# Perceiver block on one core: each batch's context loaded in two halves and its keys in two groups, each behind an event of the running batch

## What is computed

```python
def xattn(x, context, W_out, b_out, heads=16):      # keys and values are both the context itself
    q = heads_of(x); k = v = heads_of(context)
    attn = softmax(einsum('bhid,bhjd->bhij', q, k) * 32 ** -0.5)
    return merge(einsum('bhij,bhjd->bhid', attn, v)) @ W_out.T + b_out

x = x + xattn(layernorm(x), ctx_1024, W_out, b_out)
x = x + attn(layernorm(x), ...)    # latent self-attention: low-rank q and kv, rotary part, 16 heads
x = x + ffn(layernorm(x), ...)     # 8 experts, each token takes the one with the largest gate
```

## Time and profile before

| | us |
|---|---|
| median of 3 runs | 781.83 |
| lowest and highest of them | 777.88, 782.9 |
| the profiled execution, its time | 780.07 |
| its span, first to last instruction | 778.2 |
| granted clock of TensorE, mean of the span | 0.98 |

### The profile page before, as it was taken

How to read it: one execution, slowest core, us unless ns; L and a number is a source line. 1 busy time by engine, 2 the same in 40 slices (tenths; PEclk the granted TensorE clock), 3 DMA queues, 4 the chain that set the end, 5 groups by cost and what they waited for, 6 DMA issues and landing times. The chain is left out here.

```text
span 778.2 us, 26293 instructions
## 1 busy us (share of the span) xinstructions
PE 704.4 (91%) x10502; PEld 550.8 (71%) x10502; DVE 582.8 (75%) x1184; ACT 429.5 (55%) x1085; POOL 336.0 (43%) x687
## 2 busy tenths in 40 slices
PE   5899889998999999979999899999886879999997
PEld 4546668787787787868878778788775656666664
DVE  4467587887988878868888797886556647788883
ACT  3344466674766666647666576674323545555552
POOL 1122353543354435334353435443315257866542
PEclk9999899999999999989999999999998899999999
DMA  8994445545556456454664555631613996544420
GB/s 277 296 234 101 132 142 159 178 143 152 162 155 194 143 159 184 140 141 147 170 183 143 164 164 152 181 122 28 232 41 103 366 393 242 170 154 140 146 97 5
DMA packets 114378, 129.07 MB, mean 166 GB/s; under 512 B 14479, under 2 KB 81295, under 8 KB 114257
## 3 DMA queue, kind: packets, MB, share of 16 engines
q1 hardware_dynamic: 108192, 111.12, 48.2%
q0 software_dynamic: 5520, 16.26, 6.0%
q10 hardware_dynamic: 544, 0.00, 0.0%
HBM read 114.77 MB, written 14.42 MB: 166 GB/s over the span
## 5 line engine op out<-in xcount | busy, mean ns | idle before, releaser
L918 ACT ACTIVATE prob<-scores,negmax 128x257 f32<-128x257 f32 x256 | 118.3, 475 | 106.1 <-DVE negmax L1118 106.1
L1373 POOL COPY plast<-prob 128x2 f32<-128x2 f32 x128 | 24.1, 189 | 210.4 <-ACT prob L918 209.0
L560 PE MATMUL stage_banks<-qkv_hi,operand_hi 128*128 128x398 f32 x256 | 100.3, 392 | 0.2 <-DVE operand_lo L1122 0.2
L561 PE MATMUL stage_banks<-qkv_lo,operand_hi 128*128 128x398 f32 x256 | 89.0, 348 | 2.1 <-issue 2.1
L562 PE MATMUL stage_banks<-qkv_hi,operand_lo 128*128 128x398 f32 x256 | 89.1, 348 | 0.0
L1118 DVE TENSOR_REDUCE negmax<-scores 128x2 f32<-128x514 f32 x128 | 82.5, 686 | 8.7 <-PE scores L626 8.7
L1108 DVE STREAM_TRANSPOSE k_t<-keys 128x512 f32<-128x512 f32 x128 | 82.6, 685 | 2.6 <-DMA keys<-in_ctx 2.6
L1670 PE MATMUL stage_banks<-w_all,hidden 128*128 x184 | 82.8, 592 | 0.6 <-ACT hidden L1723 0.6
L636 PE MATMUL scores<-consts,prob 128*128 128x128 f32 x512 | 78.6, 278 | 1.4 <-ACT prob L918 1.0
L1766 DVE TENSOR_TENSOR w_lo<-w_all,w_hi 128x512 fp32r<-128x512 f32 x89 | 75.4, 906 | 0.2
L1113 DVE COPY prob_t<-scores 128x512 f32<-128x512 f32 x64 | 43.1, 674 | 39.5 <-PE scores L636 39.5
(11 more groups left out here) (262 smaller groups left out, 1649.5 us busy)
## 6 DMA issues: line engine op xcount, KB each, us to landing
keys<-in_ctx SPq DMA_DIRECT2D x256, 128.0 KB
context<-in_ctx SPq DMA_DIRECT2D x64, 512.0 KB, 4.0
w_all<-in_L_ffn_W SPq DMA_DIRECT2D x16, 1024.0 KB, 10.9
b<-in_L_ffn_b SPq DMA_DIRECT2D x23, 256.0 KB
norm_scratch<-norm SPq DMA_DIRECT2D x16, 256.0 KB, 3.2
x_tile<-in_x SPq DMA_DIRECT2D x8, 256.0 KB, 2.9
x_pair<-in_x SPq DMA_DIRECT2D x8, 256.0 KB, 3.0
x_scratch<-x_tile SPq DMA_DIRECT2D x8, 256.0 KB, 2.2
```

The lines of the kernel that those rows point to most:

```text
L560: pe.matmul(to, op_hi[op][:, c, :], w_hi[name][:, c, columns], start=(c == 0), stop=False)
L561: pe.matmul(to, op_hi[op][:, c, :], w_lo[name][:, c, columns], start=False, stop=False)
L918: act.activation(prob[pair][:, gg, :], scores[:, g, 0:J], ACT.Exp, bias=negmax[b % 2][:, g:g + 1], accum_out=sums[t % 2][:, g, bl:bl + 1]) ...
```

## The change

`load_context` is cut in two by partitions (64 rows of partitions each, 256 KB), and each half adds 16 to the semaphore, so `attend` waits for 32 a use. `load_keys` takes a list of the groups it is to load. In SP's loop a batch b has now: at k = 2 the first half of the context of b + 3 (behind batch b - 1 attended, as before), at k = 4 its second half (behind the exponentials of the first pair of batch b), at k = 6 two of the four DMAs of keys of b + 2 (behind all exponentials of batch b), and at k = 8 the other two (behind both turned probabilities of batch b). The wait for the keys of b to be turned stays. The loads before the loop keep their order, with eight halves of context in place of four whole ones.

```diff
-KEYS_LOAD_AT = 1
+CONTEXT_LOAD_AT, KEYS_LOAD_AT = (2, 4), (6, 8)
...
         def load_context(b):
             until.wait_ge(attended, 2 * (b - 4) + 2)
+            for half in range(2):
+                load_context_half(b, half)
+
+        def load_context_half(b, half):
+            rows = slice(half * P // 2, (half + 1) * P // 2)
             src = ins["ctx_1024"][b, 0:C2 * P, :].rearrange("(p c) d -> p c d", c=C2)
-            sp.dma_start(context[b % 4][:, :, :], src).then_inc(context_loaded[b % 4], 16)
-
-        def load_keys(b):
+            sp.dma_start(context[b % 4][rows, :, :], src[rows, :, :]).then_inc(context_loaded[b % 4], 16)
+
+        def load_keys(b, places=range(HL)):
             until.wait_ge(keys_turned, 2 * (b - 2) + 2)
-            for hl in range(HL):
+            for hl in places:
...
-            if k == 2 and 1 <= b and b + 3 < B:
-                load_context(b + 3)
-            if k == KEYS_LOAD_AT and 1 <= b and b + 2 < B:
-                load_keys(b + 2)
+            if k == CONTEXT_LOAD_AT[0] and 1 <= b and b + 3 < B:
+                until.wait_ge(attended, 2 * b)
+                load_context_half(b + 3, 0)
+            if k == CONTEXT_LOAD_AT[1] and 1 <= b and b + 3 < B:
+                until.wait_ge(exped, 4 * b + 2)
+                load_context_half(b + 3, 1)
+            if k == KEYS_LOAD_AT[0] and 1 <= b and b + 2 < B:
+                until.wait_ge(exped, 4 * b + 4)
+                load_keys(b + 2, (0, 1))
+            if k == KEYS_LOAD_AT[1] and 1 <= b and b + 2 < B:
+                until.wait_ge(prob_turned, 2 * b + 2)
+                load_keys(b + 2, (2, 3))
...
-            until.wait_ge(context_loaded[b % 4], 16 * (b // 4 + 1))
+            until.wait_ge(context_loaded[b % 4], 32 * (b // 4 + 1))
```

## The result

The changed kernel takes **807.4 us** (median of 4 runs, 805.1 to 811.0), the kernel before 782.4 us beside it (4 runs, 777.9 to 784.3): 1.034 times as long, with an interval of 1.030 to 1.039. It is slower by 25 to 27 us, and the time lies far above the range of 775 to 790.5 us. The profiled execution took 806.8 us, with a span of 805.0.

What follows compares the result with a forecast made beforehand. The prediction took PE to bound the kernel, with slack in the loads. Halves and loop keys cost 0 and batch 3's keys 1.0 us: 780.07 + 1.0 = 781.1 us, put at 782.0 towards the runs' median, range 775 to 790.5.

Steps and rivals of the forecast that it cites:

- What bounds the kernel: Attention loop: PE sets the time, busy 405.5 of 440 us, DVE and ACT close behind; the loads have slack.
- Halves, cost 0: Context loads: over 20 us of lead in the loop; four more issues before it hidden, otherwise 1.3 us.
- The keys of batch 3, 1.0 us: Preparation: two key loads behind ten small loads; DVE waits 2.6 us, PE loses 0.8, bounds 0 to 2.8, taken 1.0.
- Second, first and third batches' keys: Loop: keys land before DVE turns them, margins 1.0 us (second), 3.1 (first), no less for the third; cost 0.
- Fourth batch's keys, late by 0.4 us and covered: Loop: four key loads land 0.4 us late, hidden by 1.26 us of DVE idle; cost 0, uncovered 6 us.
- y - 4.1: Loop: cost per tile of the fourth batch's keys for a landing of y us, after DVE's idle time is used.
- keys late in the loop: Rival, slower: landing of 4.5 us instead of 3.2 costs 9.8 us, 790.9; at 5.3, 32 us; chance 0.17.
- The stalls: Rival, faster: PE's "issue" stalls in the loop go, up to 7.4 us back, 773.7; chance 0.20.
- Nothing moves: Rival, preparation: other slack takes up PE's 0.8 us or small loads land sooner, 780.1 us; chance 0.13.
- knot: Loop, once a tile: fourth batch's four key loads in a row behind the normed x2's store; forecast cost 0.
- What would show it: Profile signs: DVE waits 2 to 4 us near 46 us, in the loop at most 0.5 a tile; over 1 refutes.

Runs made afterwards that it cites:

- e2: Kernel before with only the contexts loaded in 64-partition halves, keys as before: 793.5 us, ratio 1.012.
- e8: Kernel that only loads contexts, no computing: whole ones at 380 GB/s, pairs of 64-partition halves at 226, pairs of column halves at 358.
- e3: Changed kernel, but each context half is 2 KB of all 128 partitions instead of 64 whole partitions: 797.5 us, ratio 1.017 to the kernel before.
- e4: Changed kernel, but the four contexts ahead of the loop are loaded whole: 798.7 us, ratio 1.017 to the kernel before.
- e7: Kernel before, with only batch 3's keys in two groups, the second behind the ten small loads: 784.2 us, ratio 1.003.
- e5: Changed kernel, but each tile's second batch from tile 1 issues the fourth batch's keys early, at step 1: 791.4 us, ratio 1.017 to the kernel before.
- e1: Kernel before with only the keys moved to their new places, contexts loaded whole: 797.2 us, ratio 1.015.
- e10: Kernel before, with batch 3's four key loads at step 17 instead of 12, still ahead of the small loads: 780.8 us, ratio 0.998.
- e9: Kernel before, with only the fourth batch's keys moved late, in two groups behind the normed x2's store: 790.2 us, ratio 1.012.
- e6: Kernel before with contexts in column halves (2 KB of all 128 partitions), keys as before: 781.9 us, ratio 1.001.

## Why the prediction was wrong, point by point

**What bounds the kernel** was read rightly: PE's loop with slack in the loads, and that the change could use up that slack. The size of the slack was what mattered, and it was taken too large in three places.

**Halves, cost 0: the step that failed outright.** It counted an extra issue (at most 1.3 us, at 0.33 us each where a half's took 0.50 in the median) and the lead of 20 us in the loop. The lead is real: in e2 the loop loses nothing. But the step never priced the bytes of a half. Ahead of the loop there is no lead, since the queue is full and the weights stand behind the contexts, and there a load that takes nearly the time of a whole one for half the bytes delays everything behind it. Four contexts stand ahead of Wu_v; at 2.25 us each for 1.28 (e8) they take 3.9 us more, which is nearly half of the 8.5 us by which that weight landed later. The other half is not taken apart. e2 puts the whole at 9.5 us (1.012), e3 and e4 at 9 to 14 from the other side, e8 shows the rate itself. The trace of before had only whole contexts, so a bound was wanted here and none was given.

**The keys of batch 3, 1.0 us.** Place and mechanism were right: DVE waits from 45.3 us on (e7), and PE behind it. bias_out landed at 49.1 us, as forecast. The wait was mis-sized, 5.2 us for 2.6: the last key load landed 1.4 us behind bias_out and not with it (the upper bound allowed 2), and DVE came to it 1.1 us sooner than in the kernel before. PE lost 3.3 to 3.7 us for 0.8. In time it is worth 2.5 us alone (e7), and in the changed kernel nearly nothing is left of it beside the slower halves, where DVE waited 0.9 us. This is the term that the sum was built on, and the smallest of the three.

**Second, first and third batches' keys, margins of 1.0 us and more** held. Their landing was 3.43 us in the middle and the forecast 3.2, and DVE waited for none of them but once, for 0.5 us.

**Fourth batch's keys, late by 0.4 us and covered: the step that failed in the loop.** The order was as forecast, timeline of SP of the changed kernel:

```profile
288.40 0.34 SPq L472 DMA_DIRECT2D x_tile<-in_x  x1
288.78 0.43 SPq L552 DMA_DIRECT2D norm_scratch<-norm  x1
289.31 2.64 SPq L464 DMA_DIRECT2D keys<-in_ctx  x4
292.37 1.81 SPq L457 DMA_DIRECT2D context<-in_ctx  x2
```

and DVE behind it:

```profile
297.02 1.31 DVE L1121 STREAM_TRANSPOSE k_t<-keys 128x512 f32<-128x512 f32 x2 [3.01 <-DMA keys<-in_ctx]
298.25 0.65 DVE L1126 COPY prob_t<-scores 128x512 f32<-128x512 f32 x1
```

The idle time of 1.26 us ahead of the move of the probabilities is gone: that instruction follows at once. The last issue began at 291.34 and landed at 297.0, 5.7 us. The number that was wrong is the landing, 3.2 us from the start of the kernel where 5.38 was the median in the loop. It wasn't the only landing on record either: in the loop of the kernel before, the same trace's semaphore events have 3.74 us in the middle, and 4.02 for the fourth batch's keys, already ahead of the change. With 5.38 the prediction's own formula, y - 4.1, gives 1.28 us a tile; the loop lost 1.35 against e5, of which about 1.0 is left without the "issue" stalls. That it comes so close is partly luck: in e1 the formula gives 0.88 where 1.1 was lost against the kernel before, in e3 0.81 where 0.2 was. So the rival "keys late in the loop" had the mechanism, was right about the fourth batch's keys to within some 0.6 us a tile, and was given 17 in 100 on the strength of one landing. Its upper end of 5.3 us was a median in truth. The prediction leaned on four key loads being small; behind 512 KB of other traffic they landed later than a context's median of 4.0.

**The rivals.** The stalls did not go: 5.0 + 2.3 + 2.2 + 1.3 us for 5.3 + 2.1, which is 3.4 us more and over the 3 us that the prediction had named as a sign against it. They aren't shown to come from the change: over the 12 tiles they sum to 7.4 us in the kernel before, 9.2 in e10 and 5.2 in e3, one execution each. The waits for the softmax placement stayed at 1.1 to 1.2. "Nothing moves" fell.

**The sum as the runs have it**: halves 9.5 us (e2), knot 9.5 (e9), batch 3's keys 2.5 (e7), together 21.5 against 27 in the changed kernel. From the other side the knot is worth about 14 (e5 against after). The 4 to 5 us between stay open: the knot's later landing beside the halves has the right sign, but e4 against e1, which differ by just these halves, shows only about 2 us. Behind the loop the profiled execution lost some 2 us more (from batch 62 to the end 253.6 us for 251.4), with one longer wait of PE for gathered rows (8.3 for 4.0 us); no experiment separated it.

**What would show it** was right in its conditions: it named a wait of DVE for keys "by over 1 us" as what would make the forecast wrong, and that is what came. It named no sign for the halves, because it saw no risk there.

## What to carry to other kernels

Splitting a load is not free by counting issues: ask which partitions each part writes. Cut the row (every partition, fewer bytes), not the partitions, and look first at the place where the queue is full, not at the place with slack.

When a load is moved towards its use, price its landing from rows of the same queue position, behind the loads that will stand ahead of it. A landing from a quiet place is a lower bound, and if the threshold of a rival lies within 1 us of it, that rival deserves most of the chance. A wait put behind another wait in an in-order queue (here the norm store's) collects what should have been spread.

## What the runs showed of the hardware

- Loads to 64 neighbouring partitions moved 186 to 226 GB/s with the DMA engines full, loads to 128 partitions 358 to 383 (e8), whichever half of the partitions. 256 KB to one half took as long as 512 KB to all (1.26 to 1.28 us a load). In the kernel the 4 KB packets took 292 to 299 ns in the full queue of the preparation and 207 in the loop, against 165 and 159 for whole contexts.
- Loads of 2 KB a partition ran at 358 GB/s against 380 for 4 KB: 64 more loads, each with its semaphore writes, did not show in the time (e6).
- Four loads of 128 KB landed 2.7 to 3.1 us after the last issue on a quiet core and 3.5 to 4.1 behind 512 KB. In the kernels' loops the medians were 3.1 to 4.0 away from the knot and 4.8 to 5.4 in it.
- The granted clock was lower where PE had waited: 0.79 from 14 to 30 us in the changed kernel for 1.00 before, and 0.66 from 50 to 60 us in e7, where PE had waited 3.3 us, for 1.00. The marks of the preparation in the table overstate e7 (7.2 us in the trace, 2.5 in the median).
